# Sixteen of 71 expert tiles move from the expert loop into the last turns of the batch loop

## The chip, the cores and the metric

The kernel runs on one core of one Trainium2 chip. A core has TensorE (matmuls, called PE in the profile), VectorE (DVE), ScalarE (ACT), GpSimd (POOL) and SyncE (SP), which only starts transfers here. Each engine works through its own list of instructions in order, and they wait for each other by semaphores. The metric is the time of one execution on the device in microseconds (us); before the change it is 679.85 us, the median of three runs (679.73 to 680.88).

## The reference

The input is 16 batches of a 256 x 256 array. The first layer is a graph convolution with attention over time and space; the second sends each of the 4096 tokens (256 per batch, 256 values each) through the two of eight experts that its router picks.

```python
x = x + _L0_conv_ref(_gn(x), ...)      # attention, graph convolution, layer norm
x = x + _L1_conv_ref(_gn(x), ...)      # mixture of experts
# in _L1_conv_ref:
probs = softmax(x @ gate_w.T); rw, sel = top_k(probs, 2); rw = rw / sum(rw)
combine = sum(one_hot(sel, 8) * rw[..., None], axis=1)
for e in range(8):
    h = gelu(x @ w1[e].T) * (x @ w3[e].T)
    out = out + combine[:, e:e + 1] * (h @ w2[e].T)
```

## The kernel before

**The batch part.** After a preparation of all batches, `schedule` (L113) runs turns -2 to 18. Turn i works on several batches at once, at different stages: graph convolution of batch i, layer norm of batch i-1, group norm of batch i-2 and the router of batch i-3. The turns 16, 17 and 18 have no new batch: 16 still has the layer norm of batch 15, the group norm of 14 and the router of 13; 17 the group norm of 15 and the router of 14; 18 only the router of 15. On VectorE `weave` takes one step from each of several chains in turn, so that steps of one chain wait behind others'. On the other engines the order is that of the code in `turn`.

**The router.** For each batch VectorE picks two experts per token (`route_a`, `route_b`), TensorE counts the tokens per expert (`prefix`), and `route_c` (L1280) turns that into slots, sums the counts in `cnt` and writes the weights. GpSimd's `scatter` (L928) then writes the batch's tokens in four indirect transfers to `xrows`, which has a region for each expert. `landed` waits until the four have arrived.

**The tables.** Behind turn 18, VectorE makes two tables in a chain of 21 steps: for each tile of 128 rows its expert and its place in `xrows`. Eight transfers (`fill_behind`, L268, four on SyncE's queue, four on ScalarE's) write rows without meaning behind each expert's last one, so that the last tile of an expert is full.

**The expert loop.** 71 tiles. For tile t SyncE loads 128 rows (`load_tile`), TensorE transposes them (L602), VectorE copies them out (`copy_x`, L1401) and works out where the results go in two steps on one column (L1408, L1411), TensorE multiplies by two weights (`up`, L615), ScalarE takes the gelu (L816), VectorE the product (`gate`, L1413), TensorE transposes again (L623), ScalarE copies (L827), TensorE multiplies (`down`, L630), ScalarE copies out (L822), and GpSimd (`put_rows`, L958) casts the destinations to integers (L962) and writes the rows to `yrows` by an indirect transfer (L966). The destination columns are four, reused in turn: the semaphore `c_di` counts GpSimd's casts, and VectorE's first step for tile t waits for the cast of tile t-4:

```python
dve.wait_ge(c_di, t + 1)          # c_di starts at 4
V.tensor_scalar(dn[:, 0, m], xt[:, m, N + 1:N + 2], tb3[:, 0, bass.ds(t, 1)], float(TOKENS),
                ALU.not_equal, ALU.mult).then_inc(c_dd, 1)
```

**The end** loads the two results of each token, weighs and adds them, transposes back and stores.

## Time and profile before

| | us |
|---|---|
| median of three runs | 679.85 |
| profiled execution, whole | 677.07 |
| its span, first to last instruction | 675.2 |
| TensorE busy | 533.8 (79%) |
| VectorE busy | 399.5 (59%) |
| ScalarE busy | 239.0 (35%) |
| GpSimd busy | 216.7 (32%) |

All rows are from one profiled execution, and their times are counted from its first instruction. A row such as "[6.11 <-PE bank L602]" says how long the engine had been idle before it and what ended that. In the rows of windows the third number from the end is the clock that TensorE was granted, as a share of 2.4 GHz: 1.00 is 2.4 GHz and 0.50 is 1.2 GHz.

### The profile page before, as it was taken

Reading aid. Unit: us, or ns where it says so; the run is one execution under the profiler, and the core shown is the slowest. Engines: PE = TensorE matmul, PEld = TensorE weight load, DVE = VectorE, ACT = ScalarE, POOL = GpSimd, SP = SyncE. Lnnn points to the kernel's source line nnn. Section 1 sums busy time; section 2 is a strip of 40 time slices with the busy share of each in tenths; the row PEclk is TensorE's granted clock in tenths of the full one; section 3 lists DMA queues with packets and bytes.
Section 4 is the critical chain, followed back from the end, with each engine's and each line's share of the span. In section 5 each row is a group of like instructions: output and inputs, shape, how many; then the busy total and the mean of one; then the engine's idle time right before and its main releaser. Section 6 shows DMA issues by size and latency. Waiting matters only on the chain.

```text
span 675.2 us, 11949 instructions
## 1 busy us (share of the span) xinstructions
PE 533.8 (79%) x2664; PEld 358.1 (53%) x2665; DVE 399.5 (59%) x1697; ACT 239.0 (35%) x603; POOL 216.7 (32%) x283
## 2 busy tenths in 40 slices
PE   0468489999999989989883319999999999998233
PEld 0233257776666666666662205666666665665122
DVE  4654326798898888888889753333333333332265
ACT  0343044444444444444331202333333333333232
POOL 5000000324444444444445521434334343344000
PEclk9988689999999999999986559999999999999555
DMA  9900000000000000000000142222222222220696
GB/s 293 428 23 1 0 1 1 1 0 33 33 33 33 31 33 33 32 32 33 32 32 33 55 128 63 86 79 90 82 88 81 86 89 83 91 85 28 205 312 229
DMA packets 36259, 52.85 MB, mean 78 GB/s; under 512 B 4605, under 2 KB 31360, under 8 KB 35968
## 3 DMA queue, kind: packets, MB, share of 16 engines
q1 hardware_dynamic: 24816, 30.86, 14.6%
q0 software_dynamic: 6480, 16.85, 6.7%
q10 hardware_dynamic: 4928, 4.72, 2.1%
q8 instruction: 15, 0.25, 0.2%
q14 instruction: 20, 0.16, 0.1%
HBM read 30.19 MB, written 23.14 MB: 79 GB/s over the span
## 4 chain that ended last, share of the span: by engine, by line
PE 49%; DVE 32%; DMA 8%; issue 7%; ACT 2%; POOL 1%; SPq 1%; DVEq 0%; ACTq 0%; POOLq 0%
PE bank L615 18%; PE bank L630 9%; DVE vq L1000 4%; PE bank L492 4%; DMA out<-xT 4%; PE bank L377 3%; PE bank L602 2%; PE bank L623 2%; DVE work L1177 2%; DVE work L1161 2%; PE bank L459 2%; DVE vq L999 2%; DMA xs<-x_in 2%; PE bank L367 2%; DVE work L1212 1%
## 5 line engine op out<-in xcount | busy, mean ns | idle before, releaser
L615 PE MATMUL bank<-w,xT 128*128 x284 | 135.5, 600 | 2.1 <-DVE xT L1405 2.1
L1405 DVE COPY xT<-bank 128x256 f32<-128x256 f32 x71 | 30.2, 425 | 143.6 <-PE bank L602 143.6
L966 POOL DMA_INDIRECT yrows<-xT,dest x71 | 69.5, 980 | 138.7 <-ACT xT L822 132.5
L492 PE MATMUL bank<-work 128*128 128x256 f32 x384 | 97.7, 396 | 0.0
L935 POOL DMA_INDIRECT xrows<-xtok,slot x64 | 67.2, 1050 | 78.9 <-DVEq L1298 61.7
L492 PEld LDWEIGHTS bank<-work 128*128 128x128 f32 x384 | 70.3, 195 | 9.4 <-issue 1.0
L923 POOL TENSOR_TENSOR yg<-work,sml 128x512 f32<-128x512 f32 x16 | 18.0, 1123 | 177.7 <-DVE work L1212 177.7
L630 PE MATMUL bank<-w,xT 128*128 x284 | 73.3, 380 | 1.6 <-ACT xT L827 1.6
L615 PEld LDWEIGHTS bank<-w,xT 128*128 128x128 f32 x284 | 48.9, 192 | 37.5 <-issue 37.5
L816 ACT ACTIVATE xT<-bank 128x256 f32<-128x256 f32 x71 | 27.3, 384 | 95.5 <-PE bank L615 95.5
L630 PEld LDWEIGHTS bank<-w,xT 128*128 128x128 f32 x284 | 48.5, 190 | 6.2 <-issue 2.5
L602 PEld LDWEIGHTS bank<-cst,xT 128*128 128x128 f32 x142 | 20.2, 143 | 52.2 <-issue 37.2
L822 ACT COPY xT<-bank 128x256 f32 (+1 forms) x71 | 26.4, 372 | 59.7 <-PE bank L630 59.7
L664 PE MATMUL bank<-cst,xT 128*128 128x128 f32 x64 | 17.8, 433 | 29.4 <-DVE xT L1440 29.4
L602 PE MATMUL bank<-cst,xT 128*128 128x128 f32 x142 | 27.4, 275 | 14.8 <-DMA xT<-xrows 14.8
L459 PE MATMUL bank<-sg,vs 128*128 128x256 f32 x128 | 33.5, 407 | 2.3 <-ACT sg L733 2.2
L1000 DVE SCALAR_TENSOR_TENSOR vq<-vq,vr 128x2 f32<-128x2 f32 (+1 forms) x96 | 34.5, 359 | 1.2
L1161 DVE TENSOR_TENSOR work<-bank,chebs 128x768 f32<-128x768 f32 x32 | 30.2, 952 | 5.1 <-PE bank L470 5.1
L1416 DVE TENSOR_TENSOR xT<-bank,xT 128x256 f32<-128x256 f32 x71 | 30.1, 424 | 2.1 <-ACT xT L816 2.1
L753 ACT COPY work<-bank 128x384 f32<-128x384 f32 x64 | 27.3, 478 | 9.1 <-PE bank L480 9.1
L664 PEld LDWEIGHTS bank<-cst,xT 128*128 128x128 f32 x64 | 11.4, 217 | 35.7 <-issue 26.1
L480 PE MATMUL bank<-thetabd,xT 64*128 64x192 f32 x256 | 29.8, 352 | 0.0
(200 smaller groups left out, 977.8 us busy)
## 6 DMA issues: line engine op xcount, KB each, us to landing
xT<-xrows SPq DMA_DIRECT2D x71, 129.0 KB
xT<-yrows SPq DMA_DIRECT2D x32, 256.0 KB, 4.0
xs<-x_in SPq DMA_DIRECT2D x4, 1024.0 KB, 11.3
w<-w13t_in SPq DMA_DIRECT2D x1, 4096.0 KB, 18.0
out<-xT ACTq DMA_DIRECT2D x16, 256.0 KB, 3.9
w<-w2t_in SPq DMA_DIRECT2D x1, 2048.0 KB, 22.3
yrows<-xT,dest POOLq DMA_INDIRECT x71, 2.4
xrows<-xtok,slot POOLq DMA_INDIRECT x64
```

The costliest lines, as they stand in the source:

```text
L459: last = mm(bank[1][:, c * N:(c + 1) * N], vs[:, j, c * P:(c + 1) * P], sg[:, p, j], start=(j == 0), stop=(j == C - 1))
L480: last = mm(bank[4 + r][:, h * K * P // 2:(h + 1) * K * P // 2], xT[rows, b, h, c * P:(c + 1) * P], thetabd[rows, :, r * TH // 2:(r + 1) * ...
L492: last = mm(bank[6][:, h * N:(h + 1) * N], z[:, p, c, k, h], A[:, p, c, k], start=(c == 0 and k == 0), stop=(c == C - 1 and k == K - 1))
L602: last = nc.tensor.transpose(bank[k % 2][:, c * P:(c + 1) * P], xt[:, k % SLOTS, c * P:(c + 1) * P], ident)
L615: last = mm(bank[2 + q][:, :], xc[:, q, c], w13[:, e, c].rearrange("p w n -> p (w n)"), start=(c == 0), stop=(c == C - 1))
L630: last = mm(bank[4 + q][:, 0:N], hT[:, q, f], w2[:, e, f], start=(f == 0), stop=(f == C - 1))
L935: pool.indirect_dma_start(xrows, bass.IndirectOffsetOnAxis(ap=slot[:, q, w, k:k + 1], axis=0), xtok[:, q, k], None).then_inc(sc_done[q], 16)
L966: pool.indirect_dma_start(yrows, bass.IndirectOffsetOnAxis(ap=dest[:, q], axis=0), yo[:, q], None, bounds_check=2 * TOKENS - 1, oob_is_err ...
L1000: yield from step.then(V.scalar_tensor_tensor(out=v[:, 3], in0=v[:, 2], scalar=-0.5, in1=guess, op0=ALU.mult, op1=ALU.mult))
L1161: ins = V.tensor_tensor(A[:, p, c], p3, chebs[:, c], ALU.mult)
L1405: V.tensor_copy(xc[:, q].rearrange("p c k -> p (c k)"), bank[q][:, 0:C * P]).then_inc(c_xc, 1)
L1416: V.tensor_tensor(hh[:, q].rearrange("p f k -> p (f k)"), bank[2 + q][:, C * P:2 * C * P], gl[:, q].rearrange("p f k -> p (f k)"), ALU.mul ...
```

## The change

The counts after eight batches (batches 0 to 7, taken in turn 10 as `cnt0`) give the number of full tiles per expert that are sure to be complete. From them a first table of 23 entries is made in turn 15, woven into the other chains. Tiles 0 to 15 are read from it. Their work is cut into steps of the software pipeline: step n transposes tile n, does the down product of tile n-3, the hidden transposes of tile n-2 and the up product of tile n. Steps 0 to 4 stand in turn 16, 5 to 9 in turn 17, 10 to 12 in turn 18, and 13 to 18 behind it. In these steps the tiles use the PSUM banks 1, 4, 5, 6 and 7, which are free by then. The second table leaves out what the first one gave out (`used0`); on VectorE it is woven with steps 13 to 18. The loop runs tiles 16 to 70. GpSimd's rows of the early tiles stand between its scatters: one ahead of batch 13's, five ahead of batch 14's, three ahead of batch 15's, seven behind. The router's exponential, sum, reciprocal and product become a tanh and two products with 0.5; ScalarE loads the gelu's table in turn 16 instead of behind turn 18.

```diff
+EARLY = 16
+SNAP = 8
+LATE = RUN - EARLY
 @@ sync
+            sp.wait_ge(early_tables, 1)
+            for q in range(2):
+                sp.wait_ge(sc_done[q], 16 * 2 * TT * (SNAP // 2))
+            for t in range(EARLY):
+                if t < SLOTS:
+                    load_tile(t, t)
+                else:
+                    refill(t, t % SLOTS)
             sp.wait_ge(fill_rows, 1)
             fill_behind(sp, range(E // 2))
...
 @@ tensor
+            def early_step(n):
+                if n == 0:
+                    pe.wait_ge(ld_m, 32)
+                    pe.wait_ge(early_tables, 1)
...
+                if n < EARLY:
+                    transpose_rows(n, n, n // SLOTS, True)
+                if n >= 3:
+                    down(n - 3, (n - 3) % 2, held[n - 3], True)
+                if 2 <= n < EARLY + 2:
+                    turn_hidden(n - 2, n % 2, True)
+                if n < EARLY:
+                    up(n, n % 2, held[n], True)
+
+            def early(i, k):
+                if i >= B:
+                    early_step(5 * (i - B) + k)
             def turn(i, q, ahead2, ahead1, now, back1, back2, back3):
                 if back3:
                     tokens(i - 3, 1 - q)
+                early(i, 0)
...
                 if back3:
                     turn_logits(i - 3, 1 - q)
+                early(i, 1)
...
                     gn_mean(i - 2, q)
+                    early(i, 2)
...
                     gn_var(i - 2, q)
+                    early(i, 3)
...
                     prefix(i - 3, 1 - q)
+                early(i, 4 if back2 else 2)
...
+            for n in range(13, EARLY + 3):
+                early_step(n)
             pe.wait_ge(tables, 1)
+            pe.wait_ge(c_y, EARLY + START)
 @@ scalar
-                nc.scalar.activation(r2[:, 9], r2[:, 4], ACT.Exp).then_inc(s["b_ex"], 1)
+                nc.scalar.activation(r2[:, 9], r2[:, 4], ACT.Tanh, scale=-0.5).then_inc(s["b_ex"], 1)
...
+                if n >= 3:
+                    copy_y(n - 3, (n - 3) % 2, True)
+                if 2 <= n < EARLY + 2:
+                    copy_hidden(n - 2, n % 2, True)
+                if n < EARLY:
+                    gelu(n, n % 2, True)
...
             fill_behind(act, range(E // 2, E))
+            for n in range(13, EARLY + 3):
+                early_step(n)
 @@ gpsimd
+            def early_rows(t):
+                put_rows(t, t % 4)
+                if t >= 3:
+                    pool.wait_ge(c_st[(t - 3) % 4], 16 * ((t - 3) // 4 + 1))
+                    pool.sem_inc(c_out, 1)
             def turn(i, q, ahead2, ahead1, now, back1, back2, back3):
                 if not isinstance(i, int) or i >= 4:
                     landed(q, i - 4)
                 if back1:
                     ln_out(i - 1, 1 - q)
+                if i == B:
+                    early_rows(0)
+                if i == B + 1:
+                    for t in range(1, 6):
+                        early_rows(t)
+                if i == B + 2:
+                    for t in range(6, 9):
+                        early_rows(t)
                 if back3:
                     scatter(i - 3, 1 - q)
             landed((B - 1) % 2, B - 1)
+            for t in range(9, EARLY):
+                early_rows(t)
 @@ vector
-                V.tensor_scalar(r2[:, 7], r2[:, 9], 1.0, None, ALU.add)
+                V.tensor_scalar(wts[:, b, 0], r2[:, 9], 0.5, 0.5, ALU.mult, ALU.add)
-                V.reciprocal(wts[:, b, 0], r2[:, 7])
+                V.tensor_scalar(wts[:, b, 1], r2[:, 9], -0.5, 0.5, ALU.mult, ALU.add)
-                V.tensor_tensor(wts[:, b, 1], r2[:, 9], wts[:, b, 0], ALU.mult)
...
+            def early_step(n):
+                if n < EARLY:
+                    copy_x(n, n % SLOTS, True)
+                    yield
+                if 1 <= n < EARLY + 1:
+                    gate(n - 1, (n - 1) % 2, True)
+                    yield
...
+            weave(late_table(), rest())
```

On GpSimd, from the last layer norm (L926 before, L994 after) on, `xrows<-xtok,slot` is a scatter of a batch, `dest<-xT` the cast of a tile's destinations and `yrows<-xT,dest` its store. Before, three scatters and then the tiles:

```order
L926 TENSOR_TENSOR xs<-xs,yg 128x512 [waits p_x1]
L935 DMA xrows<-xtok,slot 33920x258 [waits b_slot,b_tkc]
L935 DMA xrows<-xtok,slot 33920x258 x3
L935 DMA xrows<-xtok,slot 33920x258 [waits sc_done1,b_slot,b_tkc]
L935 DMA xrows<-xtok,slot 33920x258 x3
L935 DMA xrows<-xtok,slot 33920x258 [waits sc_done0,b_slot,b_tkc]
L935 DMA xrows<-xtok,slot 33920x258 x3
L962 CAST dest<-xT 128x1 [waits sc_done1,c_de]
```

After, the same place, from the last layer norm to the cast of tile 2:

```order
L994 TENSOR_TENSOR xs<-xs,yg 128x512 [waits p_x1]
L1016 CAST dest<-xT 128x1 [waits c_de]
L1020 DMA yrows<-xT,dest 8320x256 [waits c_y,c_di]
L1003 DMA xrows<-xtok,slot 33920x258 [waits b_slot,b_tkc]
L1003 DMA xrows<-xtok,slot 33920x258 x3
L1016 CAST dest<-xT 128x1 [waits sc_done1,c_de]
L1020 DMA yrows<-xT,dest 8320x256 [waits c_y,c_di]
L1016 CAST dest<-xT 128x1 [waits c_de]
```

The cast of tile 0 stands ahead of the scatter of batch 13; that of tile 1 behind it and behind the wait for its landing (`sc_done1`). Tile 6 stands in the same way behind batch 14, tile 9 behind batch 15.

On VectorE, the place is the end of turn 18: the last cast of slots (batch 15), then `fillf` and `filli` (the places of the fills) and the head of the table. Before:

```order
L1295 CAST slot<-slotf 128x4 [waits v_rt3]
L1364 TENSOR_TENSOR fillf<-cnt,cst 128x8 [waits v_rt3]
L1365 CAST filli<-fillf 128x8 [waits v_tb]
L1367 TENSOR_SCALAR nt<-cnt 128x8 [waits v_tb]
L1368 CAST ci<-nt 128x8 [waits v_tb]
```

After, with the copies of tiles 12 and 13 out of bank 1, their steps on the destinations, and the gates of tiles 11 and 12 (banks 5 and 4):

```order
L1380 CAST slot<-slotf 128x4 [waits v_rt3]
L1389 COPY xT<-bank1 128x256 [waits v_rt3,c_up,c_tr]
L1392 TENSOR_SCALAR xT<-xT,tb3 128x1 [waits c_di]
L1395 TENSOR_TENSOR xT<-xT 128x1 [waits c_dd]
L1400 TENSOR_TENSOR xT<-bank5,xT 128x256 [waits c_ht,c_gl]
L1460 TENSOR_TENSOR fillf<-cnt,cst 128x8 [waits v_cut]
L1389 COPY xT<-bank1 128x256 [waits c_up,c_tr]
L1392 TENSOR_SCALAR xT<-xT,tb3 128x1 [waits c_di]
L1395 TENSOR_TENSOR xT<-xT 128x1 [waits c_dd]
L1461 CAST filli<-fillf 128x8 [waits v_tb]
L1400 TENSOR_TENSOR xT<-bank4,xT 128x256 [waits c_ht,c_gl]
```

The cast `filli`, for which the eight fills wait, now stands behind the second wait on `c_di`, that of tile 13.

## Rows read from the trace of the kernel before

**Rows 1.** page: busy us and share of the engines; engines' shares of the chain
```profile
PE 533.8 (79%) x2664; PEld 358.1 (53%) x2665; DVE 399.5 (59%) x1697; ACT 239.0 (35%) x603; POOL 216.7 (32%) x283
...
PE 49%; DVE 32%; DMA 8%; issue 7%; ACT 2%; POOL 1%; SPq 1%; DVEq 0%; ACTq 0%; POOLq 0%
```

**Rows 2.** chain that ended last: start us, us, what
```profile
387.49 2.61 DMA xrows<-xtok,slot
...
394.79 4.99 DMA xrows<-xtok,slot
...
400.57 2.09 DMA xT<-xrows
...
418.06 1.72 PE bank L615 x4
...
617.51 1.72 PE bank L615 x4
```

**Rows 3.** windows: us, busy (x) of PE, PEld, DVE, ACT, POOL, clock, DMA, GB/s
```profile
359.56:402.71 43.15, 9.55 (x63) 6.63 (x63) 30.93 (x169) 7.25 (x15) 19.39 (x19) 0.50 0.25 77
360.20:374.70 14.50, 3.68 (x26) 2.54 (x22) 13.22 (x68) 2.77 (x6) 7.79 (x7) 0.50 0.10 37
374.70:382.80 8.10, 3.39 (x26) 2.54 (x22) 6.47 (x49) 2.15 (x5) 3.90 (x4) 0.50 0.18 65
382.80:389.40 6.60, 1.84 (x14) 1.14 (x10) 3.71 (x27) 1.05 (x3) 3.85 (x4) 0.50 0.22 80
389.40:402.70 13.30, 0.00 (x0) 0.00 (x0) 6.96 (x22) 1.28 (x1) 3.85 (x4) 0.50 0.48 130
```

**Rows 4.** timeline of VectorE: start us, us, line, operation, [idle before]
```profile
343.48 0.16 DVE L1290 TENSOR_TENSOR wts<-r,wts 128x2 f32<-128x2 f32 x1
343.56 0.17 DVE L1291 TENSOR_TENSOR rt<-rt 128x16 f32<-128x16 f32 x1
...
360.03 0.17 DVE L1295 CAST slot<-slotf 128x4 int32<-128x4 f32 x1
...
374.51 0.17 DVE L1295 CAST slot<-slotf 128x4 int32<-128x4 f32 x1
...
382.65 0.17 DVE L1295 CAST slot<-slotf 128x4 int32<-128x4 f32 x1
...
389.24 0.17 DVE L1295 CAST slot<-slotf 128x4 int32<-128x4 f32 x1
...
389.77 0.17 DVE L1365 CAST filli<-fillf 128x8 int32<-128x8 f32 x1
...
391.13 0.82 DVE L1374 TENSOR_TENSOR work<-nt,cst 128x632 f32<-128x632 f32 x1
...
397.12 0.20 DVE L1393 CAST itab<-work 128x73 int32<-128x73 f32 x1
403.43 0.42 DVE L1405 COPY xT<-bank 128x256 f32<-128x256 f32 x1 [6.11 <-PE bank L602]
...
404.01 0.16 DVE L1411 TENSOR_TENSOR xT<-xT 128x1 f32<-128x1 f32 x1
...
408.63 0.42 DVE L1416 TENSOR_TENSOR xT<-bank,xT 128x256 f32<-128x256 f32 x1
```

**Rows 5.** timeline of TensorE: before turn 16, and the loop's start
```profile
344.53 0.61 PE L529 MATMUL bank<-xn,sml 128*8 128x128 f32 x8 [1.71 <-ACT xn L772]
...
404.11 3.60 PE L615 MATMUL bank<-w,xT 128*128 x4 [0.71 <-DVE xT L1405]
...
408.76 1.98 PE L615 MATMUL bank<-w,xT 128*128 x4 [0.83 <-DVE xT L1405]
```

**Rows 6.** timeline of GpSimd, the scatter of batch 13
```profile
375.54 1.01 POOL L935 DMA_INDIRECT xrows<-xtok,slot  x1 [2.78 <-DVEq L1298]
```

**Rows 7.** timeline of ScalarE, its four fills
```profile
391.01 3.75 ACTq L271 DMA_DIRECT2D xrows<-fill  x4
```

**Rows 8.** windows, columns as in rows 3
```profile
346.00:347.00 1.00, 1.00 (x4) 0.79 (x3) 0.96 (x2) 0.35 (x1) 0.69 (x2) 0.50 0.30 107
```

More of the change, by code:

```diff
@@ L552, in prefix, with transpose_rows @@
                 mm(bank[2][:, 80:80 + E], one[:], mb[:, 1], start=False, stop=True).then_inc(s["b_pf"], 1)
+            def transpose_rows(t, k, turns, early=False):
+                pe.wait_ge(c_ld[k % SLOTS], 16 * (turns + 1))
+                pe.wait_ge(c_xc, t + START if early else t + START - 1)
+                for c in range(C):
+                    last = nc.tensor.transpose(bank[1 if early else k % 2][:, c * P:(c + 1) * P],
+                                               xt[:, k % SLOTS, c * P:(c + 1) * P], ident)
+                last.then_inc(c_tr, 1)
@@ new lines, in experts, with up @@
+            def experts(t):
+                v = pe.value_load(itab[0:1, 0, bass.ds(t, 1)], min_val=0, max_val=E ** AHEAD - 1)
+                return [(v >> (BITS * k)) & (E - 1) for k in range(AHEAD)]
+            def up(t, q, e, early=False):
+                pe.wait_ge(c_xc, t + (1 + START))
+                pe.wait_ge(c_h, t + START - 1)
+                for c in range(C):
+                    last = mm(bank[4 + q if early else 2 + q][:, :], xc[:, q, c], w13[:, e, c].rearrange("p w n -> p (w n)"),
+                              start=(c == 0), stop=(c == C - 1))
+                last.then_inc(c_up, 1)
@@ new lines, in turn_hidden, with down @@
+            def turn_hidden(t, q, early=False):
+                pe.wait_ge(c_h, t + (1 + START))
+                pe.wait_ge(c_hc, t + START if early else t + START - 1)
+                for f in range(C):
+                    last = nc.tensor.transpose(bank[6 if early else 6 + q][:, f * P:(f + 1) * P], hh[:, q, f], ident)
+                last.then_inc(c_ht, 1)
+            def down(t, q, e, early=False):
+                pe.wait_ge(c_hc, t + (1 + START))
+                pe.wait_ge(c_y, t + START if early else t + START - 1)
+                for f in range(C):
+                    last = mm(bank[7 if early else 4 + q][:, 0:N], hT[:, q, f], w2[:, e, f], start=(f == 0), stop=(f == C - 1))
+                last.then_inc(c_dn, 1)
@@ L794, in turn @@
                     route_exp(i - 3, 1 - q)
+                early(i, 3 if back2 else 2)
                 if ahead1:
@@ L802, in turn @@
                     normalise(i - 2, q)
+                    early(i, 4)
             schedule(turn)
@@ L874, in _ @@
             pool.sem_inc(c_out, 4)
+            pool.sem_inc(c_di, 4)
             nc.gpsimd.memset(gh[:], 0.0).then_inc(wkp, 1)
@@ L1350, in turn, with early, between @@
                 choice = choose()
+                def early(k):
+                    if i >= B:
+                        yield from early_step(5 * (i - B) + k)
+                def between():
+                    if i == B - 1:
+                        yield from early_table()
+                    if back2:
+                        yield from pause(4)
+                        yield from early(2)
+                        yield from pause(6)
+                        yield from early(3)
+                    else:
+                        yield from pause(3)
+                        yield from early(1)
                 weave(centre())
+                weave(early(0))
                 weave(statistics())
+                if back2:
+                    weave(early(1))
                 variance = layer_norm()
                 weave(attention(), along=(variance, choice))
-                weave(variance, group_norm(), matrices(), choice)
+                weave(variance, group_norm(), matrices(), choice, between())
+                if back2:
+                    weave(early(4))
                 weave(router(route_c))
+                if not back2:
+                    weave(early(2))
+                if i == SNAP + 2:
+                    V.tensor_copy(cnt0[:], cnt[:]).then_inc(v_cut, 1)
             dve.wait_ge(consts_ready, 1)
@@ L1413, in gate, with rest @@
[L1413 to L1422 removed]
+            def rest():
+                for n in range(13, EARLY + 3):
+                    yield from early_step(n)
@@ L1423, in _ @@
+            weave(late_table(), rest())
+            copy_x(EARLY, 0)
+            copy_x(EARLY + 1, 1)
+            gate(EARLY, 0)
+            with dve.Fori(0, (LATE - 2) // 4) as i:
                 for k in range(4):
-                    copy_x(4 * i + (k + 2), k + 2)
-                    gate(4 * i + (k + 1), (k + 1) % 2)
-            for t in range((RUN - 2) // 4 * 4 + 2, RUN):
+                    copy_x(4 * i + (k + 2 + EARLY), k + 2)
+                    gate(4 * i + (k + 1 + EARLY), (k + 1) % 2)
@@ L1427, in _ @@
+            for t in range(EARLY + (LATE - 2) // 4 * 4 + 2, RUN):
                 copy_x(t, t)
```

301 lines of the change are left out of this document (154 added, 147 removed).

## The prediction

> **What bounds the kernel now.** I read the page's busy shares first [rows 1]: TensorE is busy 533.8 of 675.2 us, no other engine above 60%. The chain that ended last then tells where TensorE is the limit. In the expert loop it is: 66 tiles lie between the L615 row at 418.06 and the one at 617.51, so a tile takes 199.45 / 66 = 3.022 us, nearly all TensorE [rows 2]. Before the loop it is not. In the windows over the tail of the batch part, TensorE is busy 9.55 of the 43.15 us from 359.56 (the tokens of batch 13) to 402.71 (the first expert transpose), all at the granted clock 0.50, which is 1.2 GHz [rows 3]. What runs there is VectorE's chain: the cast to slot numbers ends, 0.17 after its start, at 360.20 for batch 12, 374.68 for 13, 382.82 for 14 and 389.41 for 15 [rows 4]. So the three last turns take 14.5, 8.1 and 6.6 us, and the hand-over to the loop 13.3 us. The hand-over ends with the landing of the last scatter (394.79 + 4.99 = 399.78) and of the first tile (400.57 + 2.09) [rows 2].
>
> **What is saved.** The loop runs 16 tiles fewer, its rate is TensorE's and unchanged: 16 x 3.022 = 48.4 us. In every turn the weights of the router lose one VectorE instruction (the product at 343.48, the next one starts 0.08 later [rows 4]); some 13 full turns are paced by VectorE, which holds 32% of the chain [rows 1], so 1.0 us. The exponential becomes a tanh of the same size, at nothing. Everything else is what the 16 tiles cost ahead of the loop; I walk the five legs.
>
> **Leg A, the early table in turn 15.** 22 small VectorE steps are woven in. 13 stand among three other chains, ahead of the step that starts GpSimd, at 0.09 us each (two such steps start 0.08 apart at 343.48 [rows 4]), with 0.7 more for four of them on 184 elements; the last five stand alone before the slots of batch 12 at 0.2 each, 0.17 and a wait. 1.9 + 1.0 = 2.9 us later at slot 12. The first tile loads behind the table (0.8 + 2.09 as at the loop's start), about when the tokens of batch 13 are through TensorE, so that load is hidden.
>
> **Leg B, turn 16, five steps.** A tile costs VectorE 0.74 us for the copy and the two destination steps (403.43 to 404.17) and 0.42 for the gate: 1.16 [rows 4]. Five are 5.8. TensorE and VectorE are in-order and now wait for each other inside the turn. The transposes of tile 1 stand on TensorE behind the up product of tile 0, which at the low clock takes 3.60 us for its four (1.98 at the high one) [rows 5]; VectorE gets there 2.8 us early. The two group-norm means wait behind the up products of tiles 1 and 2 (0.8 and 1.6), tile 4's transposes behind the prefix of batch 13 (1.1). That is 6.3, less the 1.3 us that VectorE idled in this turn before (14.50 - 13.22 [rows 3]): 5.0. Leg B: +10.8.
>
> **Leg C, turn 17.** Here I see a new wait. A destination column is reused after four tiles, so VectorE's second step of tile 5 (`c_di`) needs GpSimd to have read that of tile 1. The order puts GpSimd's read behind the scatter of batch 13 and behind its landing. From slot to the end of that is measured: slot 13 at 374.68, first issue 375.54 [rows 4, 6]; slot 14 at 382.82, its last issue lands at 387.49 + 2.61 = 390.10 [rows 2, 4], and 0.3 for the cast: 7.6 us. All of VectorE stands behind it: the gate of tile 4, the statistics of batch 15, the choice of batch 14. After it come 11.9 us of VectorE's own work (the turn's 6.5 [rows 3] and five tiles' 5.8, less the copy of 0.4 that runs inside the wait), and waits for TensorE of 4.8: the mean behind tile 6's work 2.4, the variance 1.7, tile 9's transposes 0.6. 7.6 + 11.9 + 4.8 = 24.3 instead of 8.1: +16.2.
>
> **Leg D, turn 18, three steps.** The same wait again, tile 10 on tile 6 behind the landing of batch 14: 7.6. Then 6.8 of VectorE's work (3.7 [rows 3] and three tiles' 3.5, less 0.4) and 2.8 for the router's activation, which on ScalarE now stands behind the copies and the gelu of step 11. 17.2 instead of 6.6: +10.6.
>
> **Leg E, from slot 15 to the loop.** The wait comes a third time (tile 13 on tile 9, 7.6), and now the head of the late table is behind it: the fill addresses, made 0.5 us behind the slots before (389.77 [rows 4]), come out at +8.5. ScalarE issues its four fills (3.75 us [rows 7]) ahead of the copies that TensorE waits for: +12.4. Then copies and gelu of tile 13 to +13.6. TensorE has idled and is at the low clock: down of tile 11, the hidden transposes and up of tile 14 end at +18.5, up of tile 15 at +22.5, its gelu and gate at +23.4. The table's wide part stands behind that gate: 391.13 to 397.32 is 6.2 us before [rows 4], 0.6 less with 504 elements in place of 632: 5.6, to +29.0. Load and landing of tile 16: 0.6 + 2.09, to +31.6. Before it was 13.3: +18.3.
>
> **Sum.** 2.9 + 10.8 + 16.2 + 10.6 + 18.3 = 58.8 against 48.4 + 1.0: +9.4 us. The profiled execution took 677.07 us (the span of 675.2 and 1.9 around it), so it would be 686.5; the median of the runs shown is 679.85, 2.8 above it, and my number stands on that: 689.3 us.
>
> **Costs that the trace doesn't show.** (1) The clock with expert work between the turns. At the high clock throughout, the early steps give back some 8 us of the legs (the 2.8 of tile 1, 1.6 us on each of a few up products that are waited for, 2 to 3 in leg E); at the low one throughout, a tile is 6.0 us of TensorE and 13 of them fill the turns: up to +30. I take the high clock but for the first steps and those after each 7.6 us stall, since TensorE has 3.0 us of work per tile in turns of 17 to 25 us. (2) The last landing, 2.61 or 4.99 us after issue [rows 2]: I take 2.61, as the fills now come later; 2.4 more otherwise. (3) The waits between the engines, 6.3 + 4.8 + 2.8: from half to one and a half of that, 7 us either way. (4) The woven table steps: 1 to 4 us. (5) The SyncE queue: 16 loads stand ahead of its fills, but the last needs only tile 11, so nothing; 1 us if late.
>
> On the first: the clock was 0.50 from 346 on, after TensorE had been idle for 1.7 us until 344.5, though it was busy again by then [rows 5, 8]. The Trainium skill (TensorE: Matmul & The Clock Gate, section Why this matters for your kernels) warns of longer idle gaps than that one and sees short ones as harmless. By the page only the three stalls would cool TensorE, and the sum would be some 4 us lower, +5; by the row also the short waits do. The sum above leaves the page out.
>
> **Rivals.**
> *The work fills the gaps (faster).* For it: TensorE is idle 33.6 of the 43.15 us. If each GpSimd wait hides behind TensorE's own backlog, the three stalls of 7.6 go: 689.3 - 22.8 = 666.5. With perfect filling, from 364 (the tokens of batch 13, 2.4 late and 2.1 long) come 48.4 + 5 of its own + 5.6 for the table + 2.7 for the load: the loop starts at 425.7, 23.0 later than before, 26.4 us saved in all, 653 us. Against it: the wait stands in VectorE's queue ahead of the very copies that TensorE needs, and the destination columns allow only four tiles of lead. It is right if the span between slot 13 and slot 14 is under 17 us. 0.19 for anything faster, 0.05 for no change, which needs the legs to sum to 49 by accident.
> *The clock stays at 1.2 GHz (slower still).* Each tile then costs 6.0 us of TensorE: 13 x 3.0 less what is idle anyway, +20 over my sum: 709. For it: all 43 us of the tail are at 0.50 [rows 3]. Against it: at the loop's start five us of work with gaps of 0.7 brought 2.4 GHz back [rows 5]. 0.10.
> *It doesn't do what it says:* the early table could hold fewer than 16 full tiles. Eight batches are 4096 rows over 8 experts, so at least 32 - 7 = 25 full ones; I give it nothing.
>
> **How the numbers follow.** Forecast as worked out 0.66, low clock 0.10, faster 0.19, same 0.05. A difference under 0.2% (1.4 us) can't be told from none. Faster 0.19, same 0.05, slower 0.76. The forecast's own range, with (1) to (4) added in squares, is 680 to 700. To hold 8 in 10 it goes down into the filled gaps, to 671, and up towards the low clock, to 704.
>
> **What would show it.** Loop rate 3.02 as before, with the first tile of the loop at about 461 on the profile's clock. In the waits, VectorE's one-column step on the destinations idles three times for 5 to 6 us (what is left of 7.6 after the copy), and GpSimd's casts come right behind scatter landings. Distances between the slot casts: 25, 24 and 17 us. Fill issues start 8 us behind the last slots. I am wrong if the slots stand under 17 us apart, if those idle times are under 2 us, or if TensorE has most of the 16 tiles done before the last scatter lands.

## The result: 2.0% slower, and the profile after

The changed kernel took 693.45 us (689.56 to 696.2, four runs) against 680.37 (679.73 to 681.83, four runs) of the kernel before on the same chip: a ratio of 1.020, 95% interval [1.017, 1.023], or +13.1 us. The forecast was slower by 9.4 us, 689.3 us. The profiled execution took 691.28 us with a span of 689.5; before it was 677.07 and 675.2. One of the eleven executions of the best kernel further down took 858.5 us, at a mean granted clock of 0.64 where the others had 0.92 to 0.93; nothing here explains it, and its ratio leaves it out.

The page after, its busy times and the engines' shares of the chain that ended last (before: [rows 1]):

```profile
PE 545.4 (79%) x2664; PEld 360.4 (52%) x2665; DVE 399.5 (58%) x1708; ACT 238.8 (35%) x603; POOL 216.5 (31%) x283
...
PE 44%; DVE 34%; issue 8%; DMA 8%; ACT 2%; POOL 1%; ACTq 1%; SPq 1%; DVEq 0%; POOLq 0%
```

The work is the same (2664 matmuls, as before), but TensorE is busy 11.6 us longer: more of it ran at the low clock, above all the up products (144.1 us in place of 135.5 for the same 284 matmuls). Its share of the chain fell from 49 to 44%, VectorE's rose. So the tiles that left the loop are no cheaper; they went to where the chain is VectorE's and that of waits.

The timeline of VectorE after, one row for each batch's cast to slot numbers (`slot`, batches 11 to 15) and the long waits between them; compare [rows 4]:

```profile
345.24 0.17 DVE L1380 CAST slot<-slotf 128x4 int32<-128x4 f32 x1
...
362.12 0.17 DVE L1380 CAST slot<-slotf 128x4 int32<-128x4 f32 x1
...
370.24 0.42 DVE L1389 COPY xT<-bank 128x256 f32<-128x256 f32 x1 [3.28 <-PE bank L569]
...
375.04 0.16 DVE L1315 COPY gd<-bank 128x2 f32<-128x2 f32 x1 [2.88 <-PE bank L526]
...
379.44 0.16 DVE L1292 TENSOR_SCALAR vq<-bank 128x2 f32<-128x2 f32 x1 [2.05 <-PE bank L530]
...
387.74 0.42 DVE L1389 COPY xT<-bank 128x256 f32<-128x256 f32 x1 [0.65 <-PE bank L569]
...
389.98 0.17 DVE L1380 CAST slot<-slotf 128x4 int32<-128x4 f32 x1
...
398.72 0.21 DVE L1392 TENSOR_SCALAR xT<-xT,tb 128x1 f32<-128x1 f32 x1 [4.48 <-POOL dest L1016]
...
414.92 0.17 DVE L1380 CAST slot<-slotf 128x4 int32<-128x4 f32 x1
...
422.73 0.21 DVE L1392 TENSOR_SCALAR xT<-xT,tb 128x1 f32<-128x1 f32 x1 [5.43 <-POOL dest L1016]
...
430.72 0.17 DVE L1371 TENSOR_SCALAR wts<-r 128x2 f32<-128x2 f32 x1 [3.33 <-ACT r L825]
...
431.92 0.17 DVE L1380 CAST slot<-slotf 128x4 int32<-128x4 f32 x1
...
440.00 0.21 DVE L1392 TENSOR_SCALAR xT<-xT,tb 128x1 f32<-128x1 f32 x1 [4.27 <-POOL dest L1016]
...
440.32 0.16 DVE L1461 CAST filli<-fillf 128x8 int32<-128x8 f32 x1
```

The slots stand 16.9, 27.9, 24.9 and 17.0 us apart (before 15.9, 14.5, 8.1 and 6.6). The one-column step on the destinations (L1392) sits idle three times, 4.48, 5.43 and 4.27 us, each time ended by GpSimd's cast (`dest`). GpSimd's timeline shows what that cast stood behind, the first time:

```profile
391.01 0.97 POOL L1003 DMA_INDIRECT xrows<-xtok,slot  x1 [1.99 <-DVEq L1383]
...
394.83 0.97 POOL L1003 DMA_INDIRECT xrows<-xtok,slot  x1 [0.30 <-issue]
398.50 0.19 POOL L1016 CAST dest<-xT 128x1 int32<-128x1 f32 x1 [2.70 <-DMA xrows<-xtok,slot]
```

Four issues of a scatter (the first and the last are shown), then 2.70 us until it has landed, then the cast. TensorE's timeline has the other part, the count of batch 12, the up products of tiles 0 to 2, then the hand-over (compare [rows 5]):

```profile
360.11 0.19 PE L558 MATMUL bank<-mb,tri 128*128 128x8 bf16 x1 [4.20 <-DVE gr L1325]
...
365.88 3.78 PE L582 MATMUL bank<-w,xT 128*128 x4 [1.56 <-DVE xT L1389]
...
371.01 3.78 PE L582 MATMUL bank<-w,xT 128*128 x4 [0.80 <-DVE xT L1389]
...
377.31 1.98 PE L582 MATMUL bank<-w,xT 128*128 x4 [1.65 <-DVE xT L1389]
...
446.66 2.07 PE L597 MATMUL bank<-w,xT 128*128 x4 [8.37 <-ACT xT L841]
...
464.65 0.69 PE L569 MATMUL bank<-cst,xT 128*128 128x128 f32 x2 [5.16 <-DMA xT<-xrows]
```

The first transposes of the loop start at 464.65, forecast 461; before at 402.71. That is 61.9 later for 16 tiles less, 48.4 us. ScalarE's queue shows where the 8.37 come from:

```profile
441.55 4.11 ACTq L276 DMA_DIRECT2D xrows<-fill  x4
445.76 0.37 ACT L836 COPY xT<-bank 128x256 f32<-128x256 f32 x1 [10.29 <-issue]
```

The addresses of the fills (`filli`) are there at 440.48, 8.4 us behind the last slots (431.92 + 0.17) and right behind the third stall; ScalarE's fills start at 441.55, and the copies that TensorE needs come behind them.

The windows between the casts of slots after, columns as in [rows 3]:

```profile
362.12:389.98 27.86, 19.12 (x58) 9.87 (x57) 17.62 (x87) 7.14 (x16) 8.94 (x9) 0.75 0.21 61
389.98:414.92 24.94, 19.70 (x85) 10.98 (x84) 11.07 (x69) 7.17 (x20) 9.75 (x14) 0.95 0.24 76
414.92:431.92 17.00, 12.26 (x52) 7.09 (x50) 5.65 (x34) 3.92 (x12) 7.45 (x10) 0.80 0.24 79
431.92:464.65 32.73, 16.65 (x56) 10.08 (x57) 10.84 (x41) 5.34 (x16) 12.14 (x18) 0.89 0.23 81
```

No engine is full in any of them. VectorE idles 10.2, 13.9, 11.4 and 21.9 us, TensorE 8.7, 5.2, 4.7 and 16.1. This is a chain of waits in in-order queues and not an engine at its bound.

### The profile page after: what moved, and what is told of

The parts are those of the page before. It is cut to its first block, busy times and chain, and to the rows that moved or that the text cites. A ratio compares the mean times of both kernels' runs of the same rounds, so it can differ in the third digit from the quotient of the medians.

```text
span 689.5 us, 11769 instructions
## 1 busy us (share of the span) xinstructions
PE 545.4 (79%) x2664; PEld 360.4 (52%) x2665; DVE 399.5 (58%) x1708; ACT 238.8 (35%) x603; POOL 216.5 (31%) x283
## 3 DMA queue, kind: packets, MB, share of 16 engines
q1 hardware_dynamic: 24816, 30.86, 14.3%
## 4 chain that ended last, share of the span: by engine, by line
PE 44%; DVE 34%; issue 8%; DMA 8%; ACT 2%; POOL 1%; ACTq 1%; SPq 1%; DVEq 0%; POOLq 0%
PE bank L582 17%; PE bank L597 8%; DVE vq L1086 4%; DMA out<-xT 4%; PE bank L502 3%; PE bank L387 2%; PE bank L569 2%; DVE work L1263 2%; PE bank L469 2%; PE bank L590 2%; DVE work L1247 2%; DVE vq L1085 2%; DMA xs<-x_in 2%; PE bank L377 1%; DVE work L1298 1%
## 5 line engine op out<-in xcount | busy, mean ns | idle before, releaser
L582 PE MATMUL bank<-w,xT 128*128 x284 | 144.1, 632 | 13.1 <-DVE xT L1389 13.1
L502 PE MATMUL bank<-work 128*128 128x256 f32 x384 | 95.4, 389 | 0.0
L597 PE MATMUL bank<-w,xT 128*128 x284 | 75.7, 390 | 15.8 <-ACT xT L841 15.8
L582 PEld LDWEIGHTS bank<-w,xT 128*128 128x128 f32 x284 | 51.2, 201 | 53.4 <-issue 53.4
L502 PEld LDWEIGHTS bank<-work 128*128 128x128 f32 x384 | 68.7, 191 | 8.7 <-issue 0.8
L597 PEld LDWEIGHTS bank<-w,xT 128*128 128x128 f32 x284 | 49.5, 194 | 22.3 <-issue 18.3
L836 ACT COPY xT<-bank 128x256 f32 (+1 forms) x71 | 26.4, 372 | 75.6 <-PE bank L597 58.9
L490 PE MATMUL bank<-thetabd,xT 64*128 64x192 f32 x256 | 31.3, 366 | 0.0
L800 ACT COPY work<-bank 128x384 f32<-128x384 f32 x64 | 27.3, 478 | 10.4 <-PE bank L490 10.4
L709 PEld LDWEIGHTS bank<-cst,xT 128*128 128x128 f32 x64 | 11.4, 216 | 36.1 <-issue 25.6
```

What stands on the lines that cost most here:

```text
L490: last = mm(bank[4 + r][:, h * K * P // 2:(h + 1) * K * P // 2], xT[rows, b, h, c * P:(c + 1) * P], thetabd[rows, :, r * TH // 2:(r + 1) * ...
L502: last = mm(bank[6][:, h * N:(h + 1) * N], z[:, p, c, k, h], A[:, p, c, k], start=(c == 0 and k == 0), stop=(c == C - 1 and k == K - 1))
L582: last = mm(bank[4 + q if early else 2 + q][:, :], xc[:, q, c], w13[:, e, c].rearrange("p w n -> p (w n)"), start=(c == 0), stop=(c == C - 1))
L597: last = mm(bank[7 if early else 4 + q][:, 0:N], hT[:, q, f], w2[:, e, f], start=(f == 0), stop=(f == C - 1))
```

## The experiments

My theory was that three in-order waits cost most of it (VectorE behind GpSimd behind a landing), the table and the fills behind the last of them more, and the low clock at the start of turn 16 some. The rival was that the 13 tiles ahead of the last slots simply cost that much. Numbers of the profiles are single executions; verdicts are the ratios. The kernels behind "after" ran in groups of four, each beside its own runs of the kernel before: 679.41 us for the first four in the table, 679.98 for the next four, 677.85 for the last four. So kernels of different groups are compared by ratio. For orientation, all in one table: slot distances from batch 12 on, and the start of the loop's first transposes, both in us from the one profiled execution of each kernel.

| kernel | 12 to 13, 13 to 14, 14 to 15 | loop at | median, us | ratio, 95% |
|---|---|---|---|---|
| after | 27.9, 24.9, 17.0 | 464.65 | 693.45 | 1.020 [1.017, 1.023] |
| eight columns | 26.0, 20.4, 16.3 | 451.64 | 684.73 | 1.008 [1.005, 1.011] |
| table first | 28.0, 25.1, 17.0 | 460.07 | 687.45 | 1.0105 [1.0065, 1.0145] |
| landings later | 26.0, 22.3, 14.2 | 455.18 | 687.97 | 1.013 [1.011, 1.016] |
| all three | 29.2, 21.2, 12.5 | 451.75 | 677.59 | 0.9967 [0.9948, 0.9987] |
| and fills on SyncE | 27.9, 21.5, 14.2 | 452.47 | 675.96 | 0.9949 [0.9926, 0.9973] |
| after, 18 matmuls | 28.9, 25.0, 16.1 | 466.42 | 694.75 | 1.022 [1.0195, 1.025] |
| fills, 18 matmuls | 28.8, 21.4, 12.5 | 453.94 | 679.77 | 0.999 [0.997, 1.001] |
| router alone | | 399.10 | 678.83 | 0.9985 [0.9966, 1.0003] |
| after, no gaps | 24.4, 25.4, 16.0 | 463.16 | 689.66 | 1.017 [1.014, 1.021] |
| fills, no gaps | 24.2, 19.8, 12.5 | 446.51 | 672.81 | 0.9922 [0.9899, 0.9945] |
| fills, 12 tiles | 29.0, 21.2, 12.5 | 439.42 | 677.85 | 0.9996 [0.9974, 1.0017] |
| fills, 8 tiles | 27.9, 17.6, 8.6 | 431.05 | 686.54 | 1.012 [1.009, 1.016] |

**Eight destination columns.** The early tiles use eight columns in turn, so the wait on `c_di` asks for the cast eight tiles back. GpSimd reads its column by the same count; that part is not shown.

```diff
-            dn = over_xT(2, 4, 1)
+            dn = over_xT(2, 8, 1)
...
-                dve.wait_ge(c_di, t + 1)
+                d = t % 8 if early else m
+                if not early:
+                    dve.wait_ge(c_di, t + 1)
+                elif t >= 8:
+                    dve.wait_ge(c_di, t - 3)
...
```

> Eight destination columns for the early tiles instead of four, so that VectorE's step for tile t waits for GpSimd's cast of tile t-8. Nothing else changes. My theory (VectorE stands behind the wait on the casts, with its own chain behind it): the idle times of 4.5, 5.4 and 4.3 us ahead of that step go, slots 13 to 14 take about 21 instead of 24.9 us, the fill addresses come right behind the slots of batch 15, and the loop's first transpose comes some 7 us earlier: 686 us. The rival (the volume of the early work on TensorE and VectorE and the low clock pay for it all, and the wait only covers other waits): within 2 us of the changed kernel's 693.4.

684.73 us, 1.2% less than after. The three stalls are gone. Turn 17 is 4.6 us shorter, but turn 18 only 0.75. The landing is still in the way there, by a second route: GpSimd also hands back ScalarE's output rows (`yo`, four of them, by the semaphore `c_out`), and it does so behind the same landing. ScalarE's copy of a tile's result (L836) waits for that, TensorE is idle for 4.66 us before the down product behind it (416.63), and VectorE waits for ScalarE twice, 3.01 and 3.29 us. ScalarE's row in this run, and the second of VectorE's:

```profile
415.75 0.37 ACT L836 COPY xT<-bank 128x256 f32<-128x256 f32 x1 [6.47 <-POOLq L1029]
```

```profile
422.00 0.17 DVE L1371 TENSOR_SCALAR wts<-r 128x2 f32<-128x2 f32 x1 [3.29 <-ACT r L825]
```

The change as made has that wait too, 6.19 us until 423.43. In the profiles the loop starts 13.0 us earlier with eight columns, more than the 8.7 between the medians: 1.5 of it lie ahead of batch 11's slots, and 1.9 in turn 16 are the clock (see the runs without gaps), neither of which the edit touches.

**The late table first.** VectorE makes the late table whole before the copies and gates of steps 13 to 18.

```diff
-            weave(late_table(), rest())
+            run(late_table())
+            run(rest())
```

> On VectorE the whole second table stands ahead of the steps of tiles 13 to 15, instead of being woven with them. My theory: the stall behind the landing of batch 15 is then filled by the table, the fills leave 0.8 us behind the slots instead of 8, and ScalarE is through with its four fills before TensorE needs it: slots of batch 15 to loop 25 to 26 us instead of 32.6, 686 us. The rival (what ends the hand-over is the chain of stores of the last tiles, which waits for the landing anyway): no more than 2 us gained, 691 to 693.

687.45 us. The first two stalls stay (4.62 and 5.68), the third is gone, and the hand-over falls from 32.7 to 26.6 us. So the third stall cost by what stood behind it.

**The landings later.** GpSimd waits for the landing of a scatter behind the casts and stores of the turn's early tiles, not ahead of them.

```diff
             def turn(i, q, ahead2, ahead1, now, back1, back2, back3):
-                if not isinstance(i, int) or i >= 4:
+                if 4 <= i <= B:
                     landed(q, i - 4)
...
+                if i > B:
+                    landed(q, i - 4)
                 if back3:
                     scatter(i - 3, 1 - q)
...
-            landed((B - 1) % 2, B - 1)
             for t in range(9, EARLY):
                 early_rows(t)
+            landed((B - 1) % 2, B - 1)
```

> On GpSimd the wait for the landing of a scatter stands behind the early tiles' stores instead of ahead of them, in turns 17 and 18 and at the end. The four issues of the scatter (5 us) stay ahead of the casts, the landing (2.5 us) does not. My theory: each of the three stalls loses 2.4 us or more, and copies on ScalarE that wait for the stores come earlier too: 683 to 686 us. The rival (the low clock and the volume): less than 2 us. A third way: the stores then share their queue with the scatter that is still in flight and land later, which would give the gain back.

687.97 us, 0.7% less than after by the ratios. The three stalls are cut to 3.49, 3.69 and 2.25 and not to nothing, since the cast still stands behind the four issues of the scatter. GpSimd and VectorE in this run:

```profile
392.24 0.97 POOL L1003 DMA_INDIRECT xrows<-xtok,slot  x1 [0.30 <-issue]
393.22 0.19 POOL L1016 CAST dest<-xT 128x1 int32<-128x1 f32 x1
```

```profile
393.44 0.21 DVE L1394 TENSOR_SCALAR xT<-xT,tb 128x1 f32<-128x1 f32 x1 [3.49 <-POOL dest L1016]
```

The wait is thus two parts: the issues and the landing. The expected 2.4 us or more for each stall came out at 1.0, 1.7 and 2.0, and the expected 683 to 686 was too good.

**All three.**

> The three edits together: eight columns, table first, stores ahead of the landing waits. My theory: loop's first transpose 15 to 16 us earlier than in the changed kernel, near 449, which is 2 us under the point where 16 tiles fewer in the loop pay for themselves: 677 to 679 us, just under the kernel before (680.4). The rival: 690 or more.

677.59 us, 0.3% faster than before and 2.3% faster than after. The waits, not the tiles, made the change slower. That settles it between theory and rival: the same 16 tiles stand in the same turns. It does not show which part of the gain belongs to which edit; alone they were worth 1.2, 1.0 and 0.7%.

**And all fills on SyncE's queue.**

```diff
-            fill_behind(sp, range(E // 2))
+            fill_behind(sp, range(E))
...
-            act.wait_ge(fill_ready, 1)
-            act.wait_ge(fill_rows, 1)
-            fill_behind(act, range(E // 2, E))
```

> The three edits together, and all eight fills on SyncE's queue, none on ScalarE. With the three edits alone the kernel took 677.59 us; there ScalarE issues its four fills for 4.34 us from 429.50 and starts the copies of tile 10 only at 433.94, and TensorE's up product behind it starts at 435.37. If ScalarE's block sets the hand-over, the loop starts some 3 to 4 us earlier: 674. Rival: SyncE issues eight fills one after another (some 7.7 us) and the tile loads behind them come later, or the last landing is what the loop waits for anyway: 677 to 680.

675.96 us; its interval overlaps that of the three edits, and the hand-over is as long (26.45 against 26.51 us), so the expected 3 to 4 us did not come. ScalarE's 4.34 us of fills were cover for another wait: without them it copies tile 10 6.8 us behind the last slots in place of 8.7, now released by GpSimd:

```profile
432.79 0.37 ACT L836 COPY xT<-bank 128x256 f32<-128x256 f32 x1 [3.21 <-POOLq L1026]
```

And VectorE's next copy, which TensorE needs, stands behind the table anyway, 9.4 us behind the last slots in both kernels (the last table cast at 434.96, the copy at 435.38 in VectorE's timeline of this run):

```profile
434.96 0.19 DVE L1441 CAST itab<-work 128x57 int32<-128x57 f32 x1
435.38 0.42 DVE L1388 COPY xT<-bank 128x256 f32<-128x256 f32 x1 [0.23 <-DVE itab L1441]
```

**18 extra matmuls in turn 15.** They read what lies there and write a bank whose contents nobody uses. `WARM` is 18.

```diff
+                if i == B - 1:
+                    pe.wait_ge(s["b_zc"], 4 * B + START)
+                    for k in range(WARM):
+                        mm(bank[5][:, 0:N], ident, vs[:, 0], start=True, stop=True)
                 if back3:
                     prefix(i - 3, 1 - q)
```

> The changed kernel (693.45 us) with 18 extra matmuls of 256 columns on TensorE in turn 15, ahead of the count of tokens of batch 12, whose results nobody reads. They are to keep TensorE at 2.4 GHz for the early up products of tiles 0 and 1, which took 3.78 us at 365.88 and at 371.01 instead of 1.98. If the waits for TensorE in turn 16 are the low clock, the distance between the slots of batches 12 and 13 falls from 27.9 to 23 to 25 us, the time to 689 to 691. Rival: the clock falls again in the gaps between those and the early products, all is as before (693.5) or later by the matmuls' own 2 to 4 us (696).

694.75 us: a miss, as the rival said. The windows show why (the third number from the end is the granted clock):

```profile
364.00:366.00 2.00, 0.58 (x6) 0.35 (x4) 1.67 (x8) 1.67 (x3) 0.48 (x1) 1.00 0.37 95
366.00:368.00 2.00, 0.00 (x0) 0.00 (x0) 1.74 (x4) 0.29 (x1) 1.70 (x2) 0.73 0.19 66
368.00:370.00 2.00, 1.75 (x2) 0.84 (x3) 1.19 (x6) 0.00 (x0) 1.39 (x3) 0.50 0.18 66
```

The clock was 1.00 through the extra matmuls and fell in the 3.66 us without work before the first early up product, which took 3.78 us, as in the change without them. The matmuls themselves delayed the slots of batch 12: 19.8 us behind those of 11 instead of 16.9.

**The same 18 with the edits.**

> The three edits, all fills on SyncE's queue, and the 18 extra matmuls of turn 15. If both additions are worth what their own runs are to show (3.5 and 3 us), 671; if the clock falls again in the gaps and SyncE's queue becomes the wait, 678 to 681.

679.77 us, 3.8 us above the kernel without them in the same group. Again they only cost.

**No gaps.** 10 extra matmuls in turn 15, and 5, 3, 4 and 3 behind the transposes of tiles 0 to 3, where TensorE waits for VectorE's copy.

```diff
+GAPS = {0: 5, 1: 3, 2: 4, 3: 3}
...
                 if n < EARLY:
                     transpose_rows(n, n, n // SLOTS, True)
+                for k in range(GAPS.get(n, 0)):
+                    mm(bank[(5, 5, 6, 7)[n]][:, 0:N], ident, vs[:, 0], start=True, stop=True)
```

> The changed kernel with 10 extra matmuls (0.44 us each at the high clock, read from the run with 18 of them) ahead of the count of tokens of batch 12, and 5, 3, 4 and 3 more behind the transposes of tiles 0 to 3, so that TensorE has no idle time over about 1 us from 355 to the up product of tile 3. With 18 matmuls in turn 15 alone the granted clock was 1.00 up to 366 and then, after 3.66 us without work, 0.50 at the up products of tiles 0 and 1 (3.78 us each). If that gap was the cause, the up products of tiles 0 to 2 take 1.98 us now and the slots of batches 12 and 13 stand 24 to 26 us apart in place of 27.9; the time is 690 to 692. Rival: the low clock is not what turn 16 waits for, and the slots stay 27.5 to 28.5 apart, the time 693.5 or above.

689.66 us, ratio 1.017 (after 1.020; the intervals overlap). The step that it was made for is clear in the profile. TensorE's up products of tiles 0 and 1, and VectorE's first three waits:

```profile
367.51 1.98 PE L584 MATMUL bank<-w,xT 128*128 x4 [0.29 <-DVE xT L1397]
...
370.91 1.88 PE L584 MATMUL bank<-w,xT 128*128 x4
```

```profile
369.81 0.42 DVE L1397 COPY xT<-bank 128x256 f32<-128x256 f32 x1 [1.23 <-PE bank L571]
...
372.94 0.16 DVE L1323 COPY gd<-bank 128x2 f32<-128x2 f32 x1 [1.22 <-PE bank L528]
...
377.35 0.16 DVE L1300 TENSOR_SCALAR vq<-bank 128x2 f32<-128x2 f32 x1 [2.05 <-PE bank L532]
```

1.98 and 1.88 in place of 3.78 each; the waits of turn 16 sum to 5.4 with the fourth of 0.90, in place of 8.9; and the slots stand 24.36 apart in place of 27.86. The two differences are 3.5 us both. That alone could be luck, since turn 16 took from 26.0 to 29.2 us in the profiles without these matmuls. But all twelve kernels with early tiles line up by one number, the time of the first three up products together: 5.8 us in the two without gaps (turn 16 takes 24.2 and 24.4), 7.7 with eight columns and with landings later (26.0 both), 9.5 in four others (27.9 to 28.0), 10.4 to 10.6 in the last four (28.8 to 29.2). So what the low clock adds to these products, turn 16 is longer by. Some of it was given back: the slots of batch 12 came 1.1 us later behind those of batch 11, and the hand-over took 33.7 us. On the time of the whole kernel the gain is not shown.

**No gaps with the edits.** The best version found.

> The three edits (eight destination columns, the late table first, the landings waited for behind the early stores), all fills on SyncE's queue, and the extra matmuls of the run before. If the clock is worth 2 to 3 us of turn 16, 673 to 674; if it is worth nothing, the 675.96 of the same kernel without the extra matmuls, or 1 to 2 more.

672.81 us, ratio 0.992 [0.990, 0.9945]: 5 us faster than before, and 2.7% faster than the change as it was made. The gain over the same kernel without the extra matmuls, 0.27% by the ratios, is less than the two intervals tell apart (its other ten executions took 670.8 to 674.61); in the profiles the loop starts 6.0 us earlier (446.51 against 452.47), 3.7 of it in turn 16.

**Twelve and eight early tiles**, with the edits and the fills on SyncE's queue.

> The three edits and the fills on SyncE's queue, with 12 early tiles in place of 16 and 59 in the loop. Four more tiles in the loop cost 12.1 us. The last slots come 1.2 us earlier (one tile of VectorE's work less in turn 18). With 16 tiles the late table was done at 435.15 and the loop's first transposes started at 452.47, behind the six last steps; with 12 two steps are left behind the table, and the loop can start at the table's end, a load of 2.7 and 1.2 earlier, at 439 to 440. Then 12.1 - 12.8: the same time, 675 to 676. If tiles that fill the hand-over are nearly free, it is slower: 680 or more.

> As the run before with 8 early tiles and 63 in the loop: 24.2 us more in the loop than with 16. Out of turn 17 go two tiles and out of turn 18 three. If a tile costs a late turn what VectorE takes for it, 1.2 us, and a share of the waits, the slots of batch 15 come 6 to 9 us earlier and the loop starts at 431 to 434: 24.2 - 20 = some 4 us slower than with 16, 680. If the tiles in the turns cost as much as in the loop (3.0 us) or more, no slower: 676 or below.

With 12 the ratio is 0.9996, with 16 it was 0.9949: some 3 us lost, where I expected none; the two profiled spans differ by 0.3 us only (677.0 and 676.7), so whether the last four tiles pay stays open. The loop did start at 439.42 as expected. With 8 the ratio is 1.012: slower than all 71 tiles in the loop, by a median of 8.7 us (its executions lie at 682.4 to 682.6 and at 686.3 to 687.2, and the profiled one is of the first kind), where I expected 4 us more than with 16 and found some 12 by the ratios. The slot distances say how the price is made up. Turn 16 takes 27.9 us with 8 tiles as with 16: the first five tiles pay for the low clock and the waits of a chain that begins. The tiles after that are cheap: with two more tiles turn 17 grows from 17.6 to 21.5, with three more turn 18 from 8.6 to 14.2, though the same three tiles left it at 12.5 in three other profiles. That is 1.3 to 2.0 us each, less than the loop's 3.02.

**The router alone**: the kernel before, only with tanh and two products.

```diff
-                nc.scalar.activation(r2[:, 9], r2[:, 4], ACT.Exp).then_inc(s["b_ex"], 1)
+                nc.scalar.activation(r2[:, 9], r2[:, 4], ACT.Tanh, scale=-0.5).then_inc(s["b_ex"], 1)
```

> The kernel before with the router's change alone: a tanh in place of the exponential, and two VectorE instructions in place of three per batch. The term of the forecast: 13 turns paced by VectorE lose 0.08 us each, -1.0 us, ratio 0.9985. From the steady turns after the change (17.16 to 17.09 us each) -0.7. Rival: the saved instruction lies in an idle time of VectorE or costs a change of ScalarE's table: 0, or later by 1 us and more.

678.83 us, -0.15% [-0.34, +0.03]: as expected, but not told apart from nothing by the times. The profile does tell the step. Two neighbouring casts of slots in full turns start at 189.34 and 206.49 before, and at 187.61 and 204.70 with the router alone: 17.15 against 17.09, 0.06 a turn, 0.8 over 13.

## Why the prediction was right, and which terms were off

**The rate of the loop** was as said: 16 x 3.022 = 48.4 us saved. **The router's 1.0** was 0.06 to 0.07 a turn, 0.8 to 0.9. In the profiled execution it does not show, since the early turns took longer: the casts of batch 11 start at 345.24 against 344.12. That is spread between executions. In the profiles of the other kernels, whose work is the same up to there, the same cast starts anywhere from 343.70 to 346.46, and at 340.98 with the router alone. A comparison of two single profiles has that much in it before the change begins.

**Leg A** was +2.9 and came out at +1.0 (16.9 against 15.9): VectorE's busy time in the turn grew by 2.5 us (15.89 against 13.39; forecast 2.9), and its idle time fell by 1.5 (0.99 against 2.52). The forecast had no idle time to give back. Of the 1.5, 1.2 were one wait for TensorE that the profile before had, in the stretch where the clock was 0.50 ([rows 8]):

```profile
350.27 0.16 DVE L1229 COPY gd<-bank 128x2 f32<-128x2 f32 x1 [1.18 <-PE bank L516]
```

That wait comes and goes with the clock: with the router alone it is 0.33 and the same turn takes 14.99 us. Measured against that turn the leg is 1.9, so part of the small +1.0 is luck of the profile before. This is the term with the largest relative error.

**Leg B** was +10.8 and came out at +13.4. VectorE's work grew by 4.4, not 5.8 (17.62 against 13.22 busy); 0.4 of that is a slip in the sum, which has five gates where the order has four (steps 1 to 4; tile 4's stands in turn 17). The waits were the mis-sized term, 3.28, 2.88, 2.05 and 0.65, or 8.9 where I had 2.8, 0.8, 1.6 and 1.1, or 6.3. The second up product still ran at the low clock (3.78 at 371.01), and I had given that to the first alone. The run without gaps brings the waits to 5.4.

Ahead of these up products TensorE sat idle for 4.20 us, from 355.91 to the count of batch 12 at 360.11, and in that stretch the granted clock went from 1.00 (until 358) to 0.50 (from 359). It was not the choice of batch 12 that it waited for. VectorE had made that at 354.90; but `prefix` first waits for `b_nb`, the end of batch 13's group norm, and that came at 359.89:

```profile
354.90 0.17 DVE L1361 TENSOR_TENSOR mb<-rt 128x16 bf16<-128x16 f32 x1
...
359.89 0.15 DVE L1325 SCALAR_TENSOR_TENSOR gr<-gd,vr 128x2 f32<-128x2 f32 x1
```

The same wait was 2.46 us before. No run took that semaphore out of the way, so what it would be worth is open. Then, in TensorE's windows after the change, the clock came back between the second and the third up product and went again later:

```profile
374.00:378.00 4.00, 2.35 (x9) 1.36 (x9) 2.08 (x17) 0.76 (x2) 0.00 (x0) 0.85 0.01 2
378.00:382.00 4.00, 2.77 (x14) 1.66 (x12) 2.50 (x25) 1.23 (x4) 0.00 (x0) 1.00 0.13 33
382.00:386.00 4.00, 1.98 (x4) 0.68 (x4) 3.83 (x11) 0.38 (x1) 2.50 (x3) 1.00 0.13 33
386.00:390.00 4.00, 2.85 (x15) 1.98 (x16) 3.17 (x16) 1.74 (x4) 2.17 (x3) 0.86 0.08 33
```

Gaps of 1.65 and 1.92 us in the first rows did not lower it; after one of 2.48 us, up to 387.14, the clock was 1.00 until 388 and 0.50 from 389 on, and the up product that ran then took 3.58. The length of a gap alone does not decide it, as two other kernels show. With eight columns the up product behind a gap of 1.92 us took 3.47; with eight tiles the one that followed a gap of 2.48 us (up to 386.92) took 1.88:

```profile
379.28 3.47 PE L582 MATMUL bank<-w,xT 128*128 x4 [1.92 <-DVE xT L1389]
```

```profile
388.63 1.88 PE L582 MATMUL bank<-w,xT 128*128 x4
```

The prediction read the row before the change ([rows 5, 8], 1.71 us idle) as a sign that every short wait cools TensorE. Some did and some did not. The Trainium skill (TensorE: Matmul & The Clock Gate, section Why this matters for your kernels) warns of gaps longer than any of these; the clock fell behind 1.92 and 2.48 us all the same, so here the rows decide. The sum by the page, +5, was further from the measured +13.1 than the +9.4 without it.

**Leg C** was +16.2 and came out at +16.8. The stall was there as worked out, and 1.0 longer: from the end of the slots' cast (390.15) to the step's start (398.72) 8.6 us, forecast 7.6, of which 3.67 was a wait for TensorE that I had put elsewhere, and 4.48 left. The scatter's last transfer took 3.44 us to land (from 394.83, in the chain that ended last), where I had taken 2.61. **Leg D** was +10.6 and came out at +10.4; the wait for the router's activation was 3.3, forecast 2.8. What the walk did not have is that ScalarE stands behind the same landing by its own buffer (6.19 us until 423.43); in this order it ran beside VectorE's stall. **Leg E** was +18.3 and came out at +19.3 (32.7, less the cast's 0.17, against 13.3): the addresses of the fills came at +8.4, forecast 8.5, and the fills delayed TensorE as described. ScalarE was through with its own at +13.6 (441.55 + 4.11 = 445.66), forecast +12.4, but that was made up again: the gate of tile 15 ended at +23.3 (454.99 + 0.42), forecast +23.4. The 1.0 came at the end, 0.2 in the table (done at 461.30, +29.2, forecast +29.0) and 0.7 in the load of tile 16, whose transposes start 3.35 behind the table, forecast 2.7.

The five legs measured are 1.0 + 13.4 + 16.8 + 10.4 + 19.3 = 60.9, forecast 58.8. With 48.4 off and 1.1 from the earlier turns, 13.6 stand at the loop's start and 14.3 at the span's end. Two errors, A too big by 1.9 and B too small by 2.6, nearly cancel, which is luck; the difference to the forecast is B's waits, legs C and E by 0.6 and 1.0, and the first turns.

**The rivals.** That the work fills the gaps is true in part once the waits are gone: the kernel is then faster than before, by 0.3%, though not by the 2% (666.5 us) that this rival gave for the case that the three stalls go. Taking the stalls away by eight columns alone was worth 1.2%, some 8 us of the 22.8, since ScalarE's wait on the same landing and the waits for TensorE stepped into their place. As a forecast for this order it failed at the point named, the wait in VectorE's queue ahead of TensorE's copies. Low clock throughout did not come: the granted clock was 0.75, 0.95, 0.80 and 0.89 in the four windows.

Whether the three waits are all that kept the gain at 0.3 to 0.8% rather than the 26 us of perfect filling was not run to its end. What remains in the best version is a wait chain of turn 16 (24.2 us) and the draining of the early tiles before the loop (26.7 us from slots to the loop).

## What to carry to other kernels

Work that is moved into another stage's idle time must be followed through every in-order queue on its way: where a buffer is handed back by an engine that has its own long waits (here a one-column buffer of VectorE's, and ScalarE's output rows, both behind a scatter and its landing), the engine that needs the buffer inherits these waits, and with it all that stands behind it. Give such a buffer the depth of the whole stretch, or put the release ahead of the wait, before you judge whether the move pays. Look for a second buffer that comes back by the same engine: it takes over where the first wait is removed. And compare single profiles only behind a point where both agree, by distances between like instructions and not by absolute times.

## What the runs showed of the hardware that was not expected

GpSimd's indirect transfers of one tile follow each other no closer than 2.0 us, though an issue is busy 0.98: behind each cast of 0.20 it sits 0.84 before the store, with nothing to wait for but that cast (stores at 432.89 and 434.92 with the fills on SyncE's queue):

```profile
432.89 0.98 POOL L1017 DMA_INDIRECT yrows<-xT,dest  x1 [0.84 <-issue]
433.87 0.20 POOL L1013 CAST dest<-xT 128x1 int32<-128x1 f32 x1
434.92 0.99 POOL L1017 DMA_INDIRECT yrows<-xT,dest  x1 [0.84 <-issue]
```

And the early up products' clock differed from run to run with the same program ahead of them: the second was 3.78 us after the change, 1.98 in the runs with eight columns and with landings later (turn 16 then 26.0 us), without any edit that bears on it. So 1.9 us of turn 16 can come and go between executions of one kernel.
